# A first row of vectors loaded once and spread over the partitions by TensorE, and a load taken out of another's wait, in a graph and feed-forward kernel

## What is computed

```python
def gat_layer(x, W, a_s, a_d, b, edge_index, concat):
    h = (x @ W).reshape(n, H, C)                       # H = 8 heads, C = 768
    alpha_s = jnp.einsum('nhc,hc->nh', h, a_s)         # attention vectors of each head
    alpha_d = jnp.einsum('nhc,hc->nh', h, a_d)
    e = jax.nn.leaky_relu(alpha_s[src] + alpha_d[dst], NEG_SLOPE)
    ...
    msg = h[src] * alpha[:, :, None]
    out = jax.ops.segment_sum(msg, dst, num_segments=n)
```

## Time and profile before

| | before |
|---|---|
| time, median of 3 runs | 350.13 us (349.7 to 350.45) |
| profiled execution: its own time | 350.13 us |
| profiled execution: span from first to last instruction | 348.3 us |
| busy share of the span: TensorE, VectorE, ScalarE, GpSimd | 97%, 50%, 20%, 11% |
| moved by DMA | 90.18 MB, 259 GB/s in the mean |

### The profile page before, as it was taken

The page is one execution under the profiler, slowest core; times in us unless marked ns, Lnnn a source line. Parts: engine busy times, 40 slices in busy tenths (PEclk is TensorE's granted clock), DMA queues, the critical chain, the costliest instruction groups (busy, mean ns, idle before and its releaser), DMA issues.

```text
span 348.3 us, 4160 instructions
## 1 busy us (share of the span) xinstructions
PE 339.1 (97%) x1575; PEld 216.2 (62%) x1578; DVE 175.8 (50%) x530; ACT 69.6 (20%) x161; POOL 39.6 (11%) x64
## 2 busy tenths in 40 slices
PE   7998999999999999999999999999999999999997
PEld 3574656565656566557555655576545698966754
DVE  3946345666657475566753744442852501172431
ACT  2012011010101010103120321013324402073120
POOL 4910000010000000232041000031230100000000
PEclk9999999999999999999999999999999999999999
DMA  8999999999892758998999667576725800000001
GB/s 265 434 373 431 425 412 422 425 429 386 291 346 91 299 246 311 432 409 301 394 430 390 266 263 265 188 277 219 271 77 222 311 7 0 2 0 3 0 0 45
DMA packets 10645, 90.18 MB, mean 259 GB/s; under 512 B 2185, under 2 KB 2838, under 8 KB 6402
## 3 DMA queue, kind: packets, MB, share of 16 engines
q1 hardware_dynamic: 8382, 84.91, 61.4%
q0 software_dynamic: 848, 3.61, 3.0%
q10 hardware_dynamic: 1396, 1.40, 1.2%
HBM read 89.53 MB, written 0.39 MB: 258 GB/s over the span
## 4 chain that ended last, share of the span: by engine, by line
PE 76%; DVE 12%; DMA 8%; issue 3%; ACT 1%; ACTq 0%; POOL 0%; DVEq 0%
PE ps L1592 11%; PE ps L1558 9%; PE ps L1528 7%; PE ps L1984 7%; DMA avec<-in_gat_a 6%; PE ps L1787 5%; PE ps L1768 4%; DVE ring L819 3%; PE ps L1657 2%; PE ps L2096 2%; PE ps L2055 2%; PE ps L2116 2%; PE ps L1580 2%; DMA ew<-in_edge_weight 2%; PE ps L1901 2%
## 5 line engine op out<-in xcount | busy, mean ns | idle before, releaser
L1558 PE MATMUL ps<-ring,xT 128*128 128x512 f32 (+1 forms) x168 | 56.8, 486 | 0.0
L1592 PE MATMUL ps<-ring,h 128*128 128x512 f32 (+1 forms) x168 | 55.6, 486 | 0.0
L1592 PEld LDWEIGHTS ps<-ring,h 128*128 128x128 f32 x168 | 31.2, 190 | 21.9 <-issue 20.1
L1558 PEld LDWEIGHTS ps<-ring,xT 128*128 128x128 f32 x168 | 30.9, 191 | 19.1 <-issue 16.9
L521 ACT ACTIVATE h<-ps 128x768 f32<-128x768 f32 (+6 forms) x24 | 13.8, 577 | 58.6 <-PE ps L1776 15.3
L827 DVE CUSTOM_DVE_ANT_0 g<-h,avec 128x768 f32<-128x768 f32 x8 | 7.7, 959 | 34.2 <-ACT h L521 17.9
L1528 PE MATMUL ps<-ring,xT 128*128 128x512 f32 (+1 forms) x72 | 24.1, 488 | 0.1
L919 DVE TENSOR_SCALAR ring<-ring,idxb,ewb 128x128 bf16<-128x128 bf16 x99 | 24.0, 320 | 0.0
L1528 PEld LDWEIGHTS ps<-ring,xT 128*128 128x128 f32 x72 | 13.4, 190 | 9.3 <-issue 8.4
L405 POOL TENSOR_TENSOR rstd<-var,mhalf 128x1 f32<-128x1 f32 x8 | 4.7, 584 | 116.6 <-DVE var L1413 53.4
L1787 PE MATMUL ps<-ring,h 128*128 128x512 f32 (+1 forms) x48 | 16.4, 492 | 0.0
(11 more groups left out here) (421 smaller groups left out, 489.7 us busy)
## 6 DMA issues: line engine op xcount, KB each, us to landing
ring<-in_gat_w SPq DMA_DIRECT2D x14, 2304.0 KB, 11.7
avec<-in_gat_a SPq DMA_DIRECT2D x9, 768.0 KB, 9.9
ring<-in_l_w SPq DMA_DIRECT2D x3, 2304.0 KB, 18.5
ring<-in_gat_w SPq DMA_DIRECT2D x6, 384.0 KB, 6.7
ring<-in_gat_w SPq DMA_DIRECT2D x2, 1152.0 KB, 11.7
ring<-in_l_w SPq DMA_DIRECT2D x2, 1152.0 KB, 12.8
ring<-in_l1f_w1a SPq DMA_DIRECT2D x1, 2304.0 KB, 12.7
ring<-in_l1f_w1b SPq DMA_DIRECT2D x1, 2304.0 KB, 10.4
```

What stands on the lines that cost most here:

```text
L1558: last = mm(ps[:, at + lo:at + hi], xT[:, c, :], w[:, c, lo:hi], start=(c == 0), stop=(c == C - 1))
L1592: last = mm(ps[:, 4 * WIN + lo:4 * WIN + hi], h2[:, par * D + c * P:par * D + (c + 1) * P], w[:, c, lo:hi], start=(n == 0 and c == 0), sto ...
```

## The change

The first `avec` is no longer loaded by a transfer to all partitions. ScalarE loads head 0's 1536 values once, as 12 rows of 128, into the first 12 partitions of a tile that VectorE has set to zero (`first_vector`, a part of `att`). TensorE multiplies each row with a column of the identity that is broadcast over 128 columns, which puts the row on all 128 partitions of PSUM: 12 matmuls of 128 columns into banks 2, 3 and 7. ScalarE copies the three banks to `avec`. The twelve matmuls and one warming matmul stand where ten warming matmuls stood. The loads of ScalarE's queue come in the order dst, vector, src, edge weights, cols; the edge weights move from the semaphore `graph_in` to `cols_in`, so VectorE's conversion of the indices waits for dst and src alone, and POOL's splitting waits for the edge weights and cols.

```diff
--- before.py
+++ after.py
@@ -196,7 +196,8 @@
         w_out_q = g3[0:BIT, 256:640].bitcast(BF16)
         bits = h2[:, 0:384].bitcast(BF16)
         bitsT = h2[:, 384:768].bitcast(BF16)
-        SMALL = 16 * 7
+        SMALL = 16 * 8
+        first_vector = att[:, 0, :]
 
 
         S = {}
@@ -359,7 +360,6 @@
             half = UNIT // 2
             w1_1 = a["gat_w1"][1:2].rearrange("o p n -> (o p) n")
             sp.dma_start(ring[:, 1, 0:half], w1_1[:, 0:half]).then_inc(S["w1_second_in"], 16)
-            load_avec(0)
             sp.dma_start(ring[:, 1, half:UNIT], w1_1[:, half:UNIT]).then_inc(S["w1_in1"], 16)
             for h in range(1, 7):
                 load_step(h, h % 2)
@@ -421,7 +421,7 @@
             link(pool.iota(steps8, [[-1, E1N]], base=E1N, channel_multiplier=0))
             pool.tensor_copy(desc[:], steps8).then_inc(s("constants"), 1)
 
-            pool.wait_ge(S["graph_in"], 48)
+            pool.wait_ge(S["cols_in"], 32)
             link(pool.tensor_copy(ewb[:, 0, :], ew[:, 0, :]))
             link(pool.tensor_tensor(ew[:, 1, :], ew[:, 0, :], ewb[:, 0, :], ALU.subtract))
             link(pool.tensor_copy(ewb[:, 1, :], ew[:, 1, :]))
@@ -569,13 +569,18 @@
                 head_elu(h)
 
 
-            for n, name in enumerate(("dst", "src")):
-                act.dma_start(idx[:, n, :], a[name]).then_inc(S["graph_in"], 16)
-            act.dma_start(ew[:, 0, :], a["edge_weight"]).then_inc(S["graph_in"], 16)
+            act.dma_start(idx[:, 0, :], a["dst"]).then_inc(S["graph_in"], 16)
+            act.wait_ge(S["dve_step"], 1)
+            act.dma_start(first_vector[0:12, :], a["gat_a"][0:1, :].rearrange("o (k n) -> (o k) n", n=P)).then_inc(S["small_in"], 16)
+            act.dma_start(idx[:, 1, :], a["src"]).then_inc(S["graph_in"], 16)
+            act.dma_start(ew[:, 0, :], a["edge_weight"]).then_inc(S["cols_in"], 16)
             act.dma_start(cols[:], a["cols"]).then_inc(S["cols_in"], 16)
             act.wait_ge(s("constants"), 1)
             nc.scalar.activation(cell("scrap"), mhalf[:], ACT.Exp)
 
+            for n in range(3):
+                act.wait_ge(S["avec_in"], (4, 8, 16)[n])
+                copy(avec[:, n * WIN:(n + 1) * WIN], bank((2, 3, 7)[n]))
             part_T(1)
             head_rows(0, 0)
             step(0, 0)
@@ -805,12 +810,14 @@
                     .then_inc(s("T_inner_ready"), 1)
 
 
+            nc.vector.memset(first_vector, 0.0).then_inc(S["dve_step"], 1)
+            used["dve_step"] += 1
             dve.wait_ge(S["x_in"], 16)
             for n in range(2):
                 statistics(n, x)
             normalise(1, xn, x, "xn_ready")
 
-            dve.wait_ge(S["graph_in"], 48)
+            dve.wait_ge(S["graph_in"], 32)
             link(nc.vector.tensor_copy(idxb[:], idx[:]))
             dve.wait_ge(s("constants"), 3)
             iota_rows = iotab.unsqueeze(1).broadcast_to([P, EC, P])
@@ -898,7 +905,7 @@
             link(nc.vector.tensor_copy(count[:], bank(3, P)))
             link(nc.vector.tensor_scalar(absent[:], count[:], 1.0, None, ALU.min))
             link(nc.vector.tensor_scalar(absent[:], absent[:], BIG, -BIG, ALU.mult, ALU.add))
-            dve.wait_ge(S["cols_in"], 16)
+            dve.wait_ge(S["cols_in"], 32)
             head_softmax(0, 0)
             head_alphas(1, 1)
             head_z(0)
@@ -1610,7 +1617,13 @@
                 head_second(h - 1, 1 - par, w2_value).then_inc(S["w2_used"], 1)
 
             pe.wait_ge(s("constants"), 1)
-            stay_warm(10)
+            pe.wait_ge(S["small_in"], 16)
+            for k in range(12):
+                last = mm(bank((2, 3, 7)[k // 4], P, k % 4 * P), ident[:, k:k + 1].broadcast_to([P, P]), first_vector,
+                          start=True, stop=True)
+                if k % 4 == 3:
+                    last.then_inc(S["avec_in"], (4, 4, 8)[k // 4])
+            stay_warm(1, 0)
             transpose_rows(xn, "xn_ready", in_halves(1))
 
             w = ring[:, 0, :].rearrange("p (c n) -> p c n", c=C)
```

## The result

The changed kernel takes 352.39 us in the median (351.5 to 353.23, 5 runs) against 349.7 us (349.06 to 350.45, 5 runs) of the kernel before. The ratio is 1.0066, with an interval of 1.004 to 1.0093: slower by 0.66%, 2.3 us, and clear of no change. The profiled execution took 353.23 us with a span of 351.4 us; that of before had 350.13 and 348.3 us. The 1.83 us around the span are the same in both, so the two traces differ by 3.1 us, and all of it must be found in them. That is more than the medians differ by, 2.7 us, since the profiled execution of the changed kernel was the slowest of its five.

What follows compares the result with a forecast made beforehand. TensorE's unbroken queue of work was taken to bound the kernel, so a delay of its first product reaches the end. 350.13 + 2.9 (later first product) - 1.2 (waits removed) = 351.8 us; range 350.8 to 353.4.

Steps and rivals of the forecast that it cites:

- The bound: TensorE from its first product on: one queue of work, so a later start moves the end equally, barring few waits.
- The landing of the vector: Opening, ScalarE's queue: head 0's 12 short rows are in at 4.2 us, first matmul at 4.3 us.
- The price of the passes: TensorE's opening: twelve products are 24 passes of 0.22 us at the low clock, 5.3 us.
- The clock: Opening: rise at 10.0 us or 7.8 us, delaying the first product by d = 3.1 or 2.2; taken as 2.9 us.
- ScalarE's third copy: Opening, before the first xT copy: delays it 0.15 us at the high clock, costs nothing at the low one.
- The edge weights and indices: VectorE's index conversion: up to 1.5 us earlier, but the next instruction waits for the transposes, so no gain.
- The gain: Waits at head 1's score row and line 1572 vanish through an earlier second avec: 0.97 + 0.2 = 1.2 us.
- The worse row: Second avec load: 3.4 us beside its bytes, as for dst, putting avec in at 27.1 + d.
- Two of the prediction's signs: Head 1's score row: no wait above 0.2 us; VectorE's wait before the reduction ends with ScalarE's copy, not avec.
- the 0.2 us at line 1572: TensorE's wait at 67.69 us, behind the avec of head 3: goes too, with avec early by 1 us.
- the stall stays: Score row of head 1: second avec no earlier against TensorE, only d left, 353.0 us; chance 8%.
- The rival on the other side, an early clock: Opening: clock rises soon after the first real matmul, d shrinks below the gain, down to 349.4 us; chance 13%.

Runs made afterwards that it cites:

- Experiments 2: Changed kernel with the twelve 32-bit products replaced by twelve one-pass transposes of a broadcast column, head 0's attention vectors left out: 350.36 us, ratio 1.0007.
- experiment 9: Changed kernel with the twelve products and ScalarE's copies moved behind the product of head 0 and ten warming matmuls back: 351.36 us, ratio 1.0037.
- experiment 1: Changed kernel with five warming matmuls put ahead of TensorE's wait for the vector: 351.36 us, ratio 1.0044 to the kernel before.
- experiment 4: Kernel before without the first avec load, GpSimd setting avec to zero instead, warming kept: 349.42 us, ratio 0.9979.
- experiments 5 and 6: Kernel before with head 2's load halved around the second avec load, alone and with edge weights out of the indices' wait: ratios 1.0009 and 1.0014.
- experiment 3: Kernel before with only the edge weights taken out of the indices' wait: ratio 1.001.

## Why the prediction was right, and where it was off

The forecast was slower, 351.8 us, +1.7; measured are +2.7 in the medians and +2.3 by the ratio, inside the range of 350.8 to 353.4 and of the sign that was given 84%. The two terms of the sum did not do equally well, and that the median fell even into the narrower band of 351.1 to 352.7 is luck: the terms as the traces have them, 3.2 and 0.1 us, give 353.2.

- **The bound.** That TensorE's queue carries any delay of its first product to the end held: 3.22 us at 11 us are 3.10 at 70.79 us and 3.1 at the end.
- **The landing of the vector** was taken at 4.2 us and is 1.17 + 3.16 = 4.33; TensorE begins at 4.47 instead of 4.3. The fixed cost that the prediction took from the Trainium skill, DMA: Bandwidth & Descriptors, section Anatomy of one DMA, would have put it at 3.2, an estimate; that section gives its 2.0 us for transfers issued from GpSimd. This one, issued from ScalarE, took 3.16 us by itself.
- **The price of the passes** was taken as 24 x 0.22 = 5.3 us and is 5.25. Experiments 2 and 9 show it from both sides: half the passes, nearly no loss; the same passes at 2.4 GHz, 2.68 us.
- **The clock.** Of the two bounds the first (rise 5.7 us after the first matmul, d = 3.1) is what the profile shows, with d = 3.22; the 0.2 us taken off it had no row behind them. But the rise is not as firm as that bound: it came between 2.8 us (experiment 9) and 6.5 us (experiment 1) after the first work. Behind the same ten warming matmuls from 2.1 us on it came at 7.68 us in the kernel before, at 7.84, 7.30 and 5.69 in experiments 4 to 6, and at 4.92 in experiment 9. That d came out so near to the bound is in part luck.
- **ScalarE's third copy** lay beside the warming matmul and held nothing up for longer than 0.1 us: it ended at 10.56, and the copy of xT began at 10.61.
- **The edge weights and indices** bring nothing, as said (experiment 3).
- **The gain is the step that failed.** It was taken as 0.97 + 0.2 = 1.2 us and is 0.25 us at the score row and 0.1 us at the end. The sum had two rows for what a load takes beside its bytes, 2.2 us from x and 3.4 us from dst, and I took the smaller one, "since x, like head 2's load, is a large transfer from an idle queue". The measured avec is in at 30.39 us; 19.08, the issue of head 2's load, and 7.9 us of bytes leave 3.4. The worse row was the right one: 27.1 + 3.22 = 30.3. What it holds is the last of the 16 shares, 1.1 us after the fifteenth; the fifteenth alone, at 29.27, would have been before ScalarE's copy and the wait would have gone. Why the last one is late stays open. Two of the prediction's signs failed with the gain: the score row waits 0.67 us, and VectorE's wait still ends with avec. What fell with it is the 0.2 us at line 1572: the avec load of head 3 went out 2.98 us later and took 13.04 instead of 12.91.

So the rival "the stall stays", given 8%, described what happened better than the forecast did, and its 353.0 us lie as near to the result. The rival on the other side, an early clock, did not occur in the profiled execution of the changed kernel; experiment 9 shows that it can. With the worse row and the first clock bound taken, the sum would have been 350.13 + 3.1 - 0.3 = 352.9 (the prediction's lower bound of 0.4 us for the gain is a slip: 27.4 - 27.1 is 0.3).

## What to carry to other kernels

Warming matmuls are free only because they wait for nothing; real work put in their place brings its own waits with it and is paid at the low clock, so count its passes at that pace against the time until the next step could begin (10 passes here, not 24). A transfer taken out of a queue is worth less than its bytes where the next load can't be issued sooner for it: 2.0 us of transfer brought 0.6 us at the score row in experiment 4, and 0.25 in the changed kernel, where that load waits for the work that the change delays and the freed time turns into an idle queue. And where a load ends a wait, reckon with its last share of 16, not with its bytes: the pessimistic row belongs in the sum and not only in the range.

## What the runs showed of the hardware

- One load's 16 shares don't land together. For the second avec load the last one came up to 1.6 us after the fifteenth (27.49 after 25.86), and as little as 0.01 (27.41 after 27.40, before). With half of another load out of the way the eighth share came 4.4 and 5.1 us after the issue (experiments 5 and 6) instead of 6.6, and the last 7.4 and 7.8 instead of 8.2. The Trainium skill, DMA: Bandwidth & Descriptors, section Latency and other measured facts, says that two of the 16 engines are usually slower than the rest in traces, and calls its cause, which it ties to transfers issued from GpSimd, a guess; the loads here are issued from SyncE, and the increments don't tell which engine is late.
- GpSimd's three small steps on the edge weights that ran beside VectorE's one-hots took 4.55, 4.44 and 0.89 us before; in the changed kernel, where they begin ahead of the one-hots (11.27 us), they take 0.21, 0.25 and 0.21. Nobody waits for them here. The first of them, before and after:

```profile
8.27 4.55 POOL L427 CAST ewb<-ew 128x33 bf16<-128x33 f32 x1
...
10.57 0.21 POOL L427 CAST ewb<-ew 128x33 bf16<-128x33 f32 x1
```

- A pass of 128 columns of 32-bit operands takes 0.22 us at 1.2 GHz and 0.11 us at 2.4, for products (two passes) and transposes (one pass) alike: 24 in 5.25 and 2.68 us, and 12 in 2.56 at the lower level.
- The clock's rise comes at a different time in each execution: with TensorE's work the same from 2.1 us on, between 4.92 and 7.84 us in five traces.
